# The last 96 gate and 96 up rows of a feed-forward, repacked as one full tile and one 64-column tile

## The reference, cut to what matters

```python
h = _layernorm(x, axis=-1) * (1 + cb) + sb
x = x + gb * _L0_ffn_ref(h, lut, gate_idx, up_idx, down_idx)

# in _L0_ffn_ref; INTER = 1376, HIDDEN = 512, LUT_SIZE = 16
gate = x @ lut[gate_idx].T          # (tokens, 1376)
up   = x @ lut[up_idx].T
h    = silu(gate) * up
return h @ lut[down_idx].T          # (tokens, 512)
```

## Time and profile before

| | |
|---|---|
| Median of 3 runs | 1074.4 us |
| Profiled execution | 1077.47 us |
| Its span | 1075.7 us |
| TensorE busy | 973.8 us, 91% |
| VectorE, ScalarE, GpSimd busy | 55%, 38%, 16% |
| Gate and up products (L1089) | 2112 |
| Down products (L1102) | 1056 |

### The profile page before, as it was taken

How to read it: one execution, slowest core, us unless ns; L and a number is a source line. 1 busy time by engine, 2 the same in 40 slices (tenths; PEclk the granted TensorE clock), 3 DMA queues, 4 the chain that set the end, 5 groups by cost and what they waited for, 6 DMA issues and landing times.

```text
span 1075.7 us, 13315 instructions
## 1 busy us (share of the span) xinstructions
PE 973.8 (91%) x4480; PEld 472.2 (44%) x4480; DVE 590.9 (55%) x1376; ACT 410.5 (38%) x618; POOL 170.4 (16%) x151
## 2 busy tenths in 40 slices
PE   5869669967888989999898899999999999999998
PEld 5534336423333434444444444444444444444443
DVE  5599995875689873334877876322222332222212
ACT  2365764458654632225543531222222321222200
POOL 3111202003456540111201200110000001000000
PEclk9989887988998989999999999999999999999999
DMA  8658353270100011234235214222000112000011
GB/s 291 219 165 215 79 175 89 60 223 2 38 20 30 20 73 55 79 108 118 40 117 156 39 40 157 79 69 88 0 0 0 51 45 102 0 0 0 0 40 40
DMA packets 33737, 83.90 MB, mean 78 GB/s; under 512 B 2976, under 2 KB 2976, under 8 KB 30368
## 3 DMA queue, kind: packets, MB, share of 16 engines
q1 hardware_dynamic: 32544, 75.00, 21.4%
q0 software_dynamic: 1152, 8.39, 4.2%
HBM read 64.50 MB, written 18.87 MB: 78 GB/s over the span
## 4 chain that ended last, share of the span: by engine, by line
PE 69%; DVE 15%; ACT 6%; issue 6%; DMA 2%; SPq 1%; POOL 1%; ACTq 0%; DVEq 0%
PE ps L1089 32%; PE ps L1102 21%; PE ps L1056 7%; PE ps L1078 4%; PE ps L1044 2%; DVE R L802 2%; ACT R L531 2%; PE ps L1115 2%; ACT w_all L522 1%; DVE hid L780 1%; DMA w_all<-wmod_dram 1%; DVE hd L811 1%; PE ps L1068 1%; DMA hid<-idx_dram 1%; DVE xa L791 1%
## 5 line engine op out<-in xcount | busy, mean ns | idle before, releaser
L1089 PE MATMUL ps<-h,w_all 128*128 128x512 f16 x2112 | 468.3, 384 | 18.2 <-DVE hd L811 15.7
L1089 PEld LDWEIGHTS ps<-h,w_all 128*128 (+1 forms) x2112 | 208.0, 99 | 275.4 <-issue 21.1
L1102 PE MATMUL ps<-w_all,hid 128*128 128x512 f16 x1056 | 231.3, 381 | 2.3 <-DVE w_all L979 2.3
L811 DVE SCALAR_TENSOR_TENSOR hd<-ps,col,sg 128x512 f32<-128x512 f32 x88 | 65.9, 749 | 177.9 <-ACT sg L502 177.9
L1102 PEld LDWEIGHTS ps<-w_all,hid 128*128 128x128 f16 x1056 | 103.6, 98 | 127.2 <-DVE w_all L979 2.8
L502 ACT ACTIVATE sg<-ps,col 128x512 f32<-128x512 f32 x88 | 60.1, 683 | 209.0 <-PE ps L1089 208.6
L825 DVE SCALAR_TENSOR_TENSOR hd<-ps,col,gbB 128x512 f32<-128x512 f32 x32 | 24.0, 751 | 155.5 <-PE ps L1102 155.3
L407 POOL TENSOR_TENSOR h<-h,h 128x512 f16<-128x512 f32 x32 | 37.5, 1192 | 395.2 <-ACT h L487 395.2
L507 ACT ACTIVATE hid<-hd 128x512 f32 (+1 forms) x88 | 55.0, 628 | 105.6 <-DVE hd L811 105.6
L1078 PE MATMUL ps<-hid,w_all 128*128 128x512 f16 x352 | 88.6, 415 | 6.5 <-ACT w_all L522 6.5
L1056 PE MATMUL ps<-WQ,work 128*128 128x512 f16 x384 | 89.1, 395 | 4.0 <-DVE col L915 3.1
(11 more groups left out here) (102 smaller groups left out, 762.1 us busy)
## 6 DMA issues: line engine op xcount, KB each, us to landing
R<-x_dram SPq DMA_DIRECT2D x16, 1024.0 KB, 7.0
xa<-x_dram SPq DMA_DIRECT2D x15, 1024.0 KB, 6.4
hid<-idx_dram SPq DMA_DIRECT2D x44, 256.0 KB, 7.2
R<-bias_dram POOLq DMA_DIRECT2D x8, 1024.0 KB, 8.2
out_dram<-R SPq DMA_DIRECT2D x32, 256.0 KB, 2.2
x_dram<-R SPq DMA_DIRECT2D x7, 1024.0 KB, 5.1
w_all<-wmod_dram SPq DMA_DIRECT2D x6, 1024.0 KB, 15.2
h<-idx_dram SPq DMA_DIRECT2D x11, 256.0 KB, 2.6
```

Of the source, the lines that this page charges most:

```text
L811: v.scalar_tensor_tensor(hd[:, s], bank(GU[2 * s + 1]), c_kappa, sg[:, s], ALU.mult, ALU.mult) \
L1089: ins = nc.tensor.matmul(bank(GU[2 * s + t]), W[wp][:, bass.ds(at, P)], h2[hp][:, s, k], start=(k == 0 and i == 0), stop=(k == K - 1 and i ...
L1102: ins = nc.tensor.matmul(bank(QY[par]), hid[hp][:, bass.ds(at, P)], W[wp][:, w_at:w_at + BLK], start=(j == 0 and i == 0), stop=(j == J - 1 ...
```

## The change

The 96 gate and 96 up rows of the last row tile took a gate chunk and an up chunk with 32 padding rows each. They are now laid out as:

- chunk X: 64 gate rows and 64 up rows (1280 to 1343), all 128 columns full. One pass of 12 products per token block gives gate in PSUM partitions 0 to 63 and up in 64 to 127 of one bank.
- chunk Y: the remaining 32 gate and 32 up rows, 64 columns, the rest unused. These are multiplied for token block 0 with results to partitions 0 to 63 of bank `GU[1]`, and for token block 1 to partitions 64 to 127 of the same bank, one after the other in program order. A product with 64 weight columns occupies one column half of the array, and the start partition of its result says which.

Both blocks' Y products stand in the first block's unit; the second block's unit has only its X products. Silu and the multiplication take two instructions each in these units, on 64 and on 32 partitions. The hidden rows of the tile are now 0 to 31 padding, 32 to 63 from Y, 64 to 127 from X, and the down indices are permuted to match, so that the memset clears the first 32 partitions. `*_last` functions hold the new forms, and each loop ends one tile earlier. The number of chunks, the look-up of the weights and the down products are as before.

```diff
-V, HALF = LUT // 2, P // 2
+V, HALF, Q4 = LUT // 2, P // 2, P // 4
...
+            def silu_last(g, s):
+                u = (g * J + J - 1) * S + s
+                act.wait_ge(gu_ready, u + 1)
+                reach(act, hd_ready, u - 1 + s)
+                y = s * HALF
+                nc.scalar.activation(sg[HALF:P, s], bank(GU[2 * s])[0:HALF], ACT.Silu, scale=c_is[HALF:P])
+                nc.scalar.activation(sg[y + Q4:y + 2 * Q4, 0], bank(GU[1])[y:y + Q4], ACT.Silu,
+                                     scale=c_is[y:y + Q4]).then_inc(silu_ready, 1)
...
             for u in range(S * J):
                 hid_hi(0, u // S, u % S)
-                if u + 1 < S * J:
+                if u + 1 < S * (J - 1):
                     silu(0, (u + 1) // S, (u + 1) % S)
+                elif u + 1 < S * J:
+                    silu_last(0, (u + 1) % S)
...
+            def gate_units_last(g):
+                for s in range(S):
+                    silu_last(g, s)
+                    hid_hi(g, J - 1, s)
...
-                    gate_units(g, 2 + 2 * NB, J)
+                    gate_units_last(g)
                 if g > 1:
-                    gate_units(g, 0, J)
+                    gate_units(g, 0, J - 1)
+                    gate_units_last(g)
...
+            def hidden_last(g, s):
+                u = (g * J + J - 1) * S + s
+                reach(dve, hid_ready, u - 1)
+                dve.wait_ge(silu_ready, u + 1)
+                y = s * HALF + Q4
+                v.scalar_tensor_tensor(hd[HALF:P, s], bank(GU[2 * s])[HALF:P], c_kappa[HALF:P], sg[HALF:P, s],
+                                       ALU.mult, ALU.mult)
+                v.scalar_tensor_tensor(hd[Q4:HALF, s], bank(GU[1])[y:y + Q4], c_kappa[y:y + Q4], sg[y:y + Q4, 0],
+                                       ALU.mult, ALU.mult).then_inc(hd_ready, 1)
...
-                ins = v.memset(W[h][F_LAST:P, (NCH - 1) * BLK:], 0.0)
+                ins = v.memset(W[h][0:P - F_LAST, (NCH - 1) * BLK:], 0.0)
...
+            def gate_up_last(g):
+                X, Y = (2 * J - 2) * BLK, (2 * J - 1) * BLK
+                for s in range(S):
+                    u = (g * J + J - 1) * S + s
+                    reach(pe, hd_ready, u - 1)
+                    for k in range(K):
+                        for i, (wp, hp) in enumerate(SPLIT):
+                            ins = nc.tensor.matmul(bank(GU[2 * s]), W[wp][:, X + k * P:X + (k + 1) * P],
+                                                   h2[hp][:, s, k], start=(k == 0 and i == 0),
+                                                   stop=(k == K - 1 and i == 2))
+                    if s == 0:
+                        for k in range(K):
+                            for i, (wp, hp) in enumerate(SPLIT):
+                                for y in range(S):
+                                    ins = nc.tensor.matmul(bank(GU[1])[y * HALF:(y + 1) * HALF],
+                                                           W[wp][:, Y + k * P:Y + k * P + HALF],
+                                                           h2[hp][:, y, k], start=(k == 0 and i == 0),
+                                                           stop=(k == K - 1 and i == 2))
+                    ins.then_inc(gu_ready, 1)
...
-                    with pe.Fori(1, J) as j:
+                    with pe.Fori(1, J - 1) as j:
                         pe.wait_ge(w_built, 2 * j + 2)
                         for s in range(S):
                             gate_up(g, j, s)
+                    pe.wait_ge(w_built, 2 * J)
+                    gate_up_last(g)
...
-    def padded(a):
-        return np.concatenate([a, np.zeros((J * P - F,) + a.shape[1:], a.dtype)])
-    def by_channel(a):
-        return padded(a).reshape(J, P, K, P).transpose(0, 3, 2, 1)
-    down = padded(np.ascontiguousarray(down_idx.T)).reshape(J, P, K * P)
-    gate_up = np.stack([by_channel(gate_idx), by_channel(up_idx)], axis=1).reshape(2 * J, P, BLK)
+    full, half = (J - 1) * P, (J - 1) * P + HALF
+    both = lambda first, end: [gate_idx[first:end], up_idx[first:end]]
+    rows = [part for j in range(J - 1) for part in both(j * P, (j + 1) * P)]
+    rows += both(full, half) + both(half, F) + [np.zeros((HALF, C), gate_idx.dtype)]
+    gate_up = np.concatenate(rows).reshape(2 * J, P, K, P).transpose(0, 3, 2, 1).reshape(2 * J, P, BLK)
+    down_t = np.ascontiguousarray(down_idx.T)
+    pad = np.zeros((J * P - F, C), down_t.dtype)
+    down = np.concatenate([down_t[:full], pad, down_t[half:], down_t[full:half]]).reshape(J, P, K * P)
     return np.concatenate([gate_up, down])
```

More of the change, by code:

```diff
@@ L972, in _ @@
             for u in range(S * J):
-                hidden(0, u // S, u % S)
+                if u < S * (J - 1):
+                    hidden(0, u // S, u % S)
+                else:
+                    hidden_last(0, u % S)
                 if u in SELECT_AFTER:
@@ L986, in gate_units, with gate_units_last @@
                         hid_lo(g, j, s)
+            def gate_units_last(g):
+                for s in range(S):
+                    hidden_last(g, s)
+                    hid_lo(g, J - 1, s)
             for g in range(G):
@@ L1203, in _ @@
                     attn_block(NB - 1, True)
-                    for s in range(S):
-                        gate_up(g, J - 1, s)
+                    gate_up_last(g)
                 if g > 1:
-                    with pe.Fori(0, J) as j:
+                    with pe.Fori(0, J - 1) as j:
                         for s in range(S):
                             gate_up(g, j, s)
+                    gate_up_last(g)
                 pe.wait_ge(hid_ready, (g + 1) * J * S - S)
```

## The result

The changed kernel took 1066.6 us, the median of 8 runs (1064.7 to 1068.4), the kernel before 1073.3 in 8 runs beside it. The ratio is 0.9933 with a 95% interval of 0.9917 to 0.9949: 7.2 us faster, 5.5 to 8.9. The forecast was 5.5 us faster, and 1069.

The account below looks back on a forecast made before the run. TensorE's product slots were taken to bound groups two to four, a ScalarE and VectorE chain the first group's end. Three groups saving 2.22 us each (-6.66) and the first losing 1.13 gave -5.5 us: 1069 us, range 1065 to 1079.

Parts of the forecast that it names:

- A product is worth its slot in groups two to four: Gate and up products there: TensorE alone sets the pace, so each product removed saves its slot of 0.2158 us.
- A pair at 0.218 us: Half-width products of the last tile: two in different column halves take 0.218 us, 12 pairs 2.63 us a group.
- B: Half-width pairs stream together but loads stay exposed: 12 pairs take 3.78 us, total 1073.5 us; chance 0.16.
- C: Column halves do not run together: 24 half-width products take 5.18 us, loads hidden, total 1079.1 us; chance 0.12.
- D: Column halves do not run together and each load is exposed: 7.56 us a group, total 1088.6 us; chance 0.05.
- Ways in and out at 0.33 us: Changing to the half-width form and back on TensorE exposes 0.16 us of overlap twice, 0.33 us a group.
- The tail: ScalarE and VectorE after the last products: second unit's activations start 1.0 us after TensorE's end, next statistics at 5.46 us.
- the cover of 3.0 us: Slack between the next block's normalization and the transposes needing it: 3.0 us before, 0.5 us left after the change.
- The first group's wait of 4.64 us: TensorE's wait before the first group's down products, behind the padding memset: grows by 2.35 us from 2.29 us.
- The clock's further 1.0 us there: Down products behind the first group's wait: slow clock costs 1.0 us more than the 1.71 us before, bounds 0 to 1.1.
- the prediction's own sign: Test for the first group: the 66 down products behind the wait should take over 17 us.

Follow-up runs that it names:

- e1: Changed kernel with the half-width products reordered, all 12 for token block 0, then all 12 for block 1; 1.0001 of the kernel before.
- e2: Changed kernel with both blocks' half-width products in the lower column half, block 1's in its own unit and bank; 1.0018 of the kernel before.
- e7: Changed kernel with full and half-width products alternating by channel block, entering the half-width form 4 times a group instead of once; 0.9971 of the kernel before.
- e9: Changed kernel plus two more 32x512 VectorE multiplications in the last unit of the second and third groups; 0.9963 of the kernel before.

## Why the prediction came out, step by step

- **A product is worth its slot in groups two to four**: right. 48 slots became 8.00 us, all of it off the span.
- **A pair at 0.218 us**: right. 12 pairs take 2.59 us plus the way in. e1 and e2 show that it is the other half that does it, and the start times 3 to 4 ns apart that the two run at once. Rivals B (3.8 us), C (5.2) and D (7.6) are out, and the load is hidden on the same rows in the half form too.
- **Ways in and out at 0.33 us**: a little dear. They are 0.12 and 0.11, 0.23 us [e7]. With the pair this makes 2.36 saved against 2.22, 7.08 against 6.66 us for three groups. As a term the 0.33 us had no row behind it, and being near was partly luck: it stood for two overlaps of 0.16 us laid bare, and the runs show only what the two ways cost, not what happens in them.
- **The tail**: right. ScalarE's second unit starts 1.0 us after the last product (1.0 predicted), the statistics 5.34 us after (5.46), and of the cover of 3.0 us about 0.5 is left [e9], as predicted.
- **The first group's wait of 4.64 us**: right, 4.73 measured.
- **The clock's further 1.0 us there**: the step that failed. The loss was 16.06 - 14.40 = 1.66 us after 4.73 us of idle time, against 1.71 after 2.29; the prediction's own sign, over 17 us for the 66 products, read 16.06. I had read a rule of length out of two waits near 4.1 us. The other runs show that the same wait of 4.7 us cost 1.4 to 3.0 us and one of 3.7 us nothing. So the 1.66 us of this run was a draw, and the term's bounds, 0 to 1.1 us above 1.71, hold neither end of what the six runs lost. Such a term should have been a range, not a step that grows with the wait.

With these sizes the sum is -7.08 for three groups and -2.36 + 2.44 - 0.05 = 0.03 for the first: 7.05 us, beside 7.2 measured. The forecast of 5.5 was short by 1.5 us, 1.1 of it the first group (nearly all the clock) and 0.4 the ways in and out and the pair. The clock's term also set the chances: the prediction gave "faster", by more than 5.4 us, 0.41 and no change 0.46, because with it the forecast lay right at that bound.

On the two rules: for products in different column groups the Trainium skill (TensorE: Matmul & The Clock Gate, section Part 3: Packing small matmuls) says that they run concurrently, and e2 against the changed kernel agrees (12 in one half in 2.71 us, 24 in both in 2.71 us). The sentence in the same section of the Trainium skill that a load overlaps a running product only with another row group does not hold here; all 24 use the same 128 rows, and 24 loads of 0.110 us and 24 products together take 2.71 us. The Trainium skill (TensorEngine Tiling (Array Packing), section Key Properties) says that a change of mode drains the engine. e7 shows a price of 0.11 to 0.12 us a way, below the 0.16 us overlap that I had put in for it; whether the array empties in that time no run here shows.

## What to carry to other kernels

A last tile that fills half of the array's columns or less can be multiplied for two token blocks at once, and saves nearly a quarter of that tile's gate and up time (2.36 of 10.36 us); turn to the other half every three products or sooner, or the gain shrinks though nothing else changes (runs of 6 gave back 0.46 of the 2.36 us, runs of 12 1.75). Runs of 4 and 5 were not tried. Before adding instructions to the tail of a stage, look up what the next stage really waits for: here a half-microsecond memset behind the last multiplication held up products that did not need it for another 30, and moving it was worth as much as the change (7.3 and 7.2 us; in the kernel before, with its shorter wait, 4.5). And put the price of a slow clock behind a wait into a sum as a range.

## What was not expected of the hardware

- Runs of 3 products per half overlap as fully as turns of 1 (2.72 and 2.71 us), runs of 6 lose 2 slots (3.17), runs of 12 lose 8 (4.46).
- An activation or multiplication on 32 or 64 partitions takes what 128 take: 679, 680 and 683 ns, 750, 757 and 749 ns. Splitting one by partitions nearly doubles the time, here two activations of 0.68 us for one.
- The granted clock's loss after idle time varies between runs of the same wait: 1.4 to 3.0 us after 4.7 us. After 3.7 us it was nothing, after 2.3 us 1.7. What decides it stays open.
